# A recurrent layer on one core: key matrices before the small scales, an output projection in split fp16 products, and turns and updates moved or left out

## The reference

```
q, k, v = silu(conv4(xn @ Wq.T)), silu(conv4(xn @ Wk.T)), silu(conv4(xn @ Wv.T))   # 6 heads of 64
q, k = q / |q|, k / |k|                        # per head
beta = sigmoid(xn @ Wb.T);  g = -exp(A_log) * softplus(xn @ Wa.T + dt_bias)
per time step:  S = S * exp(g);  u = beta * (v - k S);  S = S + k^T u;  o = q S / 8
o = o * rsqrt(mean(o*o) + 1e-5) * o_norm_w * silu(xn @ Wg.T)
s = o @ Wo.T                                   # 384 -> 512, the output projection
f = relu(xn @ sign(up).T * up_scale) @ sign(down).T * down_scale * output_scale   # hidden 2048
x = x + s * silu(f)
```

## Time and profile before

| | us |
|---|---|
| median of 3 runs | 1397.91 (1397.85 to 1403.75) |
| the profiled execution's own time | 1397.27 |
| its span | 1395.2 |
| TensorE busy | 1330.5 (95%) |
| VectorE busy | 1065.5 (76%) |
| ScalarE busy | 734.8 (53%) |
| GpSimd busy | 524.1 (38%) |

### The profile page before, as it was taken

How to read it: one execution, slowest core, us unless ns; L and a number is a source line. 1 busy time by engine, 2 the same in 40 slices (tenths; PEclk the granted TensorE clock), 3 DMA queues, 4 the chain that set the end, 5 groups by cost and what they waited for, 6 DMA issues and landing times. The chain is left out here.

```text
span 1395.2 us, 24351 instructions
## 1 busy us (share of the span) xinstructions
PE 1330.5 (95%) x8972; PEld 652.9 (47%) x8972; DVE 1065.5 (76%) x1870; ACT 734.8 (53%) x1305; POOL 524.1 (38%) x434
## 2 busy tenths in 40 slices
PE   5888999999999999999999999999999999999998
PEld 2332333333333333333345548654585546755485
DVE  7889877787877887788857777597685886768855
ACT  5675666556655666566576423365134552354331
POOL 3599852112201321122215642176221753137331
PEclk9999999999999999999999999999999999999999
DMA  6420000000001000100460230102400013002211
GB/s 234 179 84 3 7 8 4 24 30 16 9 14 41 14 8 16 31 24 1 158 267 31 58 61 32 39 8 62 88 17 31 24 46 80 24 23 56 42 24 46
DMA packets 80469, 68.51 MB, mean 49 GB/s; under 512 B 46080, under 2 KB 67296, under 8 KB 77792
## 3 DMA queue, kind: packets, MB, share of 16 engines
q1 hardware_dynamic: 67936, 65.39, 15.2%
q10 hardware_dynamic: 12416, 1.57, 1.1%
HBM read 44.87 MB, written 17.87 MB: 45 GB/s over the span
## 5 line engine op out<-in xcount | busy, mean ns | idle before, releaser
L621 DVE TENSOR_REDUCE mS<-vpair 128x1 f16<-128x512 f32 x512 | 329.1, 686 | 112.8 <-PE vpair L1125 110.6
L936 ACT ACTIVATE probs<-bank 128x512 f16<-128x512 f32 x512 | 277.3, 595 | 163.4 <-PE bank L1132 163.1
L1179 PE MATMUL bank<-rows,both 128*128 128x512 f16 x1024 | 243.0, 380 | 0.4 <-DVE th L650 0.4
L436 POOL TENSOR_TENSOR h<-th,h 128x512 f16<-128x512 f32 x61 | 71.5, 1172 | 219.1 <-ACT h L907 219.1
L1179 PEld LDWEIGHTS bank<-rows,both 128*128 128x128 f16 x1024 | 91.3, 98 | 121.2 <-issue 15.5
L2156 PE MATMUL bank<-rows,both 128*128 128x512 f16 x512 | 117.2, 379 | 0.0
L1125 PE MATMUL vpair<-qk 32*128 32x512 f16 x512 | 99.9, 385 | 18.1 <-DVE mS L621 7.7
L2172 PE MATMUL bank<-both,hid 128*128 128x512 f16 x512 | 111.2, 379 | 0.0
L2140 PE MATMUL bank<-rows,both 128*128 128x512 f16 (+1 forms) x456 | 104.4, 379 | 0.9 <-PEq L160 0.9
L1132 PE MATMUL bank<-qv,qk 32*128 32x512 f16 x512 | 99.5, 385 | 0.0
L1193 PE MATMUL bank<-dn,h 128*128 128x512 f16 x256 | 98.0, 383 | 0.0
(11 more groups left out here) (334 smaller groups left out, 2671.9 us busy)
## 6 DMA issues: line engine op xcount, KB each, us to landing
h<-in_ug SPq DMA_DIRECT2D x8, 1024.0 KB, 5.3
lt_scratch<-big SPq DMA_DIRECT2D x16, 384.0 KB, 2.8
dn<-in_down SPq DMA_DIRECT2D x2, 2048.0 KB, 11.0
x_scratch<-th SPq DMA_DIRECT2D x16, 256.0 KB, 2.2
res<-x_scratch SPq DMA_DIRECT2D x16, 256.0 KB, 4.8
out_x<-res SPq DMA_DIRECT2D x16, 256.0 KB, 2.0
both<-in_w SPq DMA_DIRECT2D x2, 1548.0 KB, 10.4
t_scratch<-tok SPq DMA_DIRECT2D x16, 192.0 KB, 2.1
```

Source lines behind the costliest of these rows:

```text
L436: pool.tensor_tensor(h16(ft, 1), row32, h16(ft, 0), ALU.subtract).then_inc(S["row_lo"], 1)
L621: v.tensor_reduce(mS[:, u % 2, qt, 32 * j + DH:32 * j + DH + 1], SA[n % 2][:, :], AX.X, ALU.max).then_inc(S["max_done"], 1)
L936: a.activation(probs[:, n % (2 * G), :], SB[n % 2][:, :], ACT.Exp, scale=float(DH) ** -0.5).then_inc(S["p_ready"], 1)
L1179: mm = pe.matmul(GB[n % 2][:, :], w[:, kt, col:col + P], xnb(b, kt), start=r == 0, stop=r == 2 * KT - 1)
```

## The change

In the second layer:

1. `matrices("KK", 0)` runs on VectorE before the small scales instead of after them.
2. K and V of the first chunk are turned in step 0 after X5 instead of before Z. K of the last chunk is not turned or scaled, since
3. the state update after the last chunk (its decay, product and sum) is left out: nothing reads it.
4. The output projection: `wo1` is held as two fp16 halves of the scaled weights, and turned y as two fp16 halves, each projection is 9 fp16 products (high by high, high by low, low by high) instead of 3 fp32 ones. The high half of y is evicted by ScalarE, the low half by VectorE (`low_y`), so y's bank moves from ScalarE's rotation to VectorE's. A power-of-two scale for the weights is found in batch 0 on VectorE (`output_maxima`, `output_scales`, `output_low`), one TensorE product and two ScalarE operations. The weights' load is put into space of the hidden tile, and waits until the first layer's last rows are stored.

Two semaphores of the first layer are merged into others.

```diff
@@ bank_order
-        v += [(b, "bat")] + [(b - 1, "wo", TT - 1)] * (b > 0) + [(b, "ss")]
-        a += [(b, "ba"), (b, "pre", 0)] + [(b - 1, "yT", TT - 1)] * (b > 0)
+        v += [(b, "bat")] + [(b - 1, "yT", TT - 1), (b - 1, "wo", TT - 1)] * (b > 0) + [(b, "ss")]
+        a += [(b, "ba"), (b, "pre", 0)]
...
+            v += (tt > 1) * [(b, "yT", tt - 2)]
             v += (tt > 2) * [(b, "wo", tt - 3)]
-            a += (tt > 1) * [(b, "yT", tt - 2)]
-            v += rec * [(b, "SU", tt - 1)]
+            v += (rec and inv) * [(b, "SU", tt - 1)]
@@ layer1, SyncE
-            sp.dma_start(wo1[:, :, :], d["wo1"]).then_inc(S["wo_in"], 16)
+            sp.wait_ge(W["x1_last"], 32)
+            sp.dma_start(wraw, d["wo1"]).then_inc(S["wo_in"], 16)
@@ VectorE
+                def output_maxima():
+                    v.wait_ge(S["wo_in"], 16)
+                    v.tensor_reduce(wmax[:, 0:1], wraw, AX.XY, ALU.max, apply_absolute_value=True).then_inc(S["wo_r"], 1)
+                    v.tensor_reduce(wmax[:, 2:3], onw, AX.X, ALU.max, apply_absolute_value=True).then_inc(S["wo_r"], 1)
+
+                def output_scales():
+                    v.wait_ge(S["yh_r"], 1)
+                    v.wait_ge(S["wo_r"], 2)
+                    v.tensor_scalar(wmax[:, 1:3], wmax[:, 1:3], 1e-30, None, ALU.max).then_inc(S["wo_r"], 1)
+                    v.wait_ge(S["wo_r"], 3)
+                    v.tensor_scalar(wpow.bitcast(I32), wmax[:, 1:3].bitcast(I32), 0x7F800000, None, ALU.bitwise_and).then_inc(S["wo_r"], 1)
+                    v.wait_ge(S["wo_r"], 4)
+                    v.reciprocal(winv, wpow).then_inc(S["wo_r"], 1)
+                    v.tensor_scalar(wo_un, wpow[:, 0:1], wpow[:, 1:2], 0.5 / WO_TOP / Y_TOP, ALU.mult, ALU.mult).then_inc(S["wo_r"], 1)
+                    v.wait_ge(S["wo_r"], 5)
+                    v.tensor_scalar(wo_sc, winv[:, 0:1], WO_TOP, None, ALU.mult).then_inc(S["wo_r"], 1)
+                    v.tensor_scalar(y_sc, winv[:, 1:2], Y_TOP, None, ALU.mult).then_inc(S["wo_r"], 1)
+
+                def output_low():
+                    v.wait_ge(S["yh_r"], 2)
+                    v.wait_ge(S["wo_r"], WO_STEPS - 1)
+                    v.scalar_tensor_tensor(wo1[:, 1], wraw, wo_sc, wo1[:, 0], ALU.mult, ALU.subtract).then_inc(S["wo_r"], 1)
+
+                def low_y(n, rt):
+                    k = VI[n, "yT", rt]
+                    v.wait_ge(S["yh_r"], 2 + n * TT + rt + 1)
+                    v.scalar_tensor_tensor(yT[:, 1, :, rt * P:(rt + 1) * P], vbank[k % 3][:, 0:KW].rearrange("p (m c) -> p m c", m=MT), y_sc,
+                                           yT[:, 0, :, rt * P:(rt + 1) * P], ALU.mult, ALU.subtract).then_inc(S["v_took"], 1)
...
                 v.scalar_tensor_tensor(az, z[:, :, LH:], -1.0, z[:, :, LH:], ALU.mult, ALU.min).then_inc(S["az_r"], 1)
                 if b:
+                    low_y(b - 1, TT - 1)
                     gated(b - 1, TT - 1)
+                else:
+                    output_maxima()
                 conv(1)
...
                 for m in range(3, 7):
                     conv(m)
                     silu(m - 1)
+                    if b == 0 and m == 4:
+                        output_scales()
+                    if b == 0 and m == 6:
+                        output_low()
                 conv(7)
...
+                matrices("KK", 0)
                 v.wait_ge(S["v_took"], VI[b, "ss"] + 1)
                 v.reciprocal(rsk, ssq[:, :, LH:]).then_inc(S["small_r"], 1)
...
-                matrices("KK", 0)
                 matrices("KQ", 0)
...
+                    if tt > 1:
+                        low_y(b, tt - 2)
                     if tt > 2:
                         gated(b, tt - 3)
@@ ScalarE
+                def high_y(n, rt):
+                    k = VI[n, "yT", rt]
+                    a.wait_ge(S["v_full"], k + 1)
+                    a.activation(yT[:, 0, :, rt * P:(rt + 1) * P], vbank[k % 3][:, 0:KW].rearrange("p (m c) -> p m c", m=MT), ACT.Copy,
+                                 scale=y_sc).then_inc(S["yh_r"], 1)
...
+                if b == 0:
+                    a.wait_ge(S["wo_r"], WO_STEPS - 1)
+                    a.activation(wo1[:, 0], wraw, ACT.Copy, scale=wo_sc).then_inc(S["yh_r"], 1)
                 tanh_conv(5)
@@ TensorE, project_out
                     for m in range(MT):
-                        mm = pe.matmul(vbank[k % 3][:, :], yT[:, m, tt * P:(tt + 1) * P], wo1[:, m, :], start=m == 0, stop=m == MT - 1)
+                        for i, j in ((0, 0), (0, 1), (1, 0)):
+                            mm = pe.matmul(vbank[k % 3][:, :], yT[:, i, m, tt * P:(tt + 1) * P], wo1[:, j, m, :],
+                                           start=m == 0 and i == j, stop=m == MT - 1 and i == 1)
@@ TensorE, steps
                     if inv:
                         product_X5()
+                    if tt == 0:
+                        turn_kv()
...
-                    if rec:
+                    if rec and inv:
                         bk = vfill("SU", rt)
...
+                    if 0 < tt < TT:
+                        turn_kv()
                     if inv:
-                        turn_kv()
                         bk = vfill("Z", tt)
```

More of the change, by code:

```diff
@@ L1288 @@
 XRAISE, WRAISE = 64.0, 128.0
+WO_TOP, Y_TOP = 2.0 ** 14, 2.0 ** -10
+WO_STEPS = 9
+WO_COL = 3 * TT * LH
 def bank_order():
@@ L1713, in gated @@
                     v.wait_ge(S["g2_r"], n * TT + tt + 1)
-                    v.scalar_tensor_tensor(gate2(tt), split(vbank[k % 3][:, :]), 0.5, gate2(tt), ALU.mult, ALU.mult).then_inc(S["v_took"], 1)
+                    v.scalar_tensor_tensor(gate2(tt), split(vbank[k % 3][:, :]), wo_un, gate2(tt), ALU.mult, ALU.mult).then_inc(S["v_took"], 1)
                 def residual(n, tt):
@@ L1748, in _, with matrices @@
                     silu(m - 1)
+                    if b == 0 and m == 4:
+                        output_scales()
+                    if b == 0 and m == 6:
+                        output_low()
                 conv(7)
+                def matrices(nm, tt):
+                    dst = (LT if nm == "KK" else BT)[tt]
+                    for hf in range(2):
+                        v.wait_ge(S["GTm_r"], (b * TT + tt) * 2 + hf + 1)
+                        v.tensor_tensor(dst[:, hf:LH:2, :], mats(take(nm, tt, hf)), GT[tt % 2][:, hf:LH:2, :],
+                                        ALU.mult).then_inc(S["v_took"], 1)
                 bk = take("ss")[:, 0:TT * 2 * LH].rearrange("p (t c) -> p t c", t=TT)
@@ L1763, in _ @@
                 v.tensor_scalar(sn5[:, :, :], sn, rowm[:, 0:1], None, ALU.mult).then_inc(S["snm_r"], 1)
-                def matrices(nm, tt):
-                    dst = (LT if nm == "KK" else BT)[tt]
-                    for hf in range(2):
-                        v.wait_ge(S["GTm_r"], (b * TT + tt) * 2 + hf + 1)
-                        v.tensor_tensor(dst[:, hf:LH:2, :], mats(take(nm, tt, hf)), GT[tt % 2][:, hf:LH:2, :],
-                                        ALU.mult).then_inc(S["v_took"], 1)
                 def invert_blocks():
@@ L1874, in _ @@
                     if rec:
[L1876 to L1878 removed]
+                        k = b * KV + 2 * rt
+                        if inv:
+                            v.wait_ge(S["kv_full"], k + 1)
+                            v.tensor_tensor(heads(Kt), heads(fbank[0][:, 0:KW]), hb(vec[:, rt, LH:2 * LH], HD), ALU.mult).then_inc(S["kv_took"], 1)
+                            k += 1
+                        v.wait_ge(S["kv_full"], k + 1)
                         v.tensor_tensor(heads(Rv), heads(fbank[1][:, 0:KW]), hb(rvs[:, rt, :], HD), ALU.mult).then_inc(S["kv_took"], 1)
@@ L1922, in _ @@
                     if rec:
-                        v.wait_ge(S["ssS_r"], w + 1)
-                        v.tensor_tensor(S_[:, nxt, :, :], take("SU", rt)[:, 0:MT * HD].rearrange("p (h c) -> p h c", h=MT), ssS[:, :, :],
-                                        ALU.add).then_inc(S["v_took"], 1)
+                        if inv:
+                            v.wait_ge(S["ssS_r"], b * (TT - 1) + rt + 1)
+                            v.tensor_tensor(S_[:, nxt, :, :], take("SU", rt)[:, 0:MT * HD].rearrange("p (h c) -> p h c", h=MT), ssS[:, :, :],
+                                            ALU.add).then_inc(S["v_took"], 1)
                         v.wait_ge(S["osq"], w + 1)
@@ L1935, in _ @@
                 residual(b, TT - 2)
+            low_y(B - 1, TT - 1)
             gated(B - 1, TT - 1)
@@ L2028, in _ @@
                 tanh_conv(2)
+                if b == 0:
+                    a.activation(wmax[:, 1:2], take("vec")[:, WO_COL:WO_COL + 1], ACT.Copy).then_inc(S["yh_r"], 1)
                 a.activation(vec[:, :, :].rearrange("p t (i h) -> p i t h", i=3),
@@ L2152, in up_tile @@
                     else:
-                        past(pe, "kv_took", 2 * b * TT)
+                        past(pe, "kv_took", b * KV)
                     for kt in range(KT):
@@ L2177, in turn_y @@
                 def turn_y(n, rt):
```

(15 more changed lines are left out.)

50 lines of the change are left out of this document (24 added, 26 removed).

## The result

The changed kernel takes 1391.58 us (median of 7 runs, 1390.54 to 1394.60); the kernel before took 1399.89 beside it (7 runs, 1397.85 to 1403.75). The ratio is 0.9933, 95% interval 0.9918 to 0.9948: 0.7% or 8.3 us faster. The forecast was 12.2 us and 1385.7, with a range up to 1389.5: the direction was right, the time lies above the range. Of the 5.9 us between forecast and result 2.0 are the base (1399.89 instead of 1397.91 for the kernel before) and 3.9 are gain that did not come.

A forecast was written before the change was run, and what follows sets the result against it. TensorE, busy 95% of the span, was taken as the bound. Terms -10.3 - 2.0 - 1.6 - 5.1 + 1.6 + 3.3 + 0.5 + 1.4 = -12.2 us gave 1385.7 us; range 1381 to 1389.5, own range 1383 to 1388.5.

The forecast's parts named there:

- First chunk turned in the first step: Chunk step 0: six transposes move from before Z into TensorE's idle 0.55 us before Y5; taken as 0 a batch.
- Next x: Batch boundary: the next batch's first product newly waits for ScalarE's last turned copy, about 0.15 us x 3, +0.5.
- Preparation in batch 0: New VectorE maxima, tiny scale operations and low half of the weights delay batch 0; +1.6 us taken.
- rival B: Batch 0 preparation at its upper bound, each tiny operation waiting on GpSimd: +2.9, 1388.6 us; chance 0.12.
- The projections: Output projections on TensorE: 2.58 us becomes 1.94, gain 0.64 each, 16 of them, 10.3 us.
- the boundary waits: Batch boundaries: projection newly waits 1.1 us for VectorE's low half of y, 3 times, +3.3 us.
- the key matrices in batches 1 to 3: First key matrices masked ahead of the small scales: TensorE's wait goes, 1.7 us a batch, 5.1 us.
- the tail: After the last chunk: end moves 2.04 us earlier, so 1.4 of the 3.45 us priced there is not had.
- Rival C: Key wait only moves, KQ 0's masks coming as late as the old ones: +5.1, 1390.8 us; chance 0.08.
- D: No new waits, only a shorter TensorE queue; boundary, x and tail terms (5.2) fall away, 1380.5 us; chance 0.10.
- E: Low halves queue behind VectorE's next-x work, so TensorE waits at every turn of y: above 1405 us; chance 0.03.
- Rival F: Chunk steps are a VectorE and ScalarE chain; the 8.7 us taken from TensorE only opens idle time: 1394.4; chance 0.05.

The follow-up runs named there:

- best: Changed kernel with boundary projection after pre_tile(2), first chunk's K and V turned before Z again, idle products in the tail's two gaps; 1383.39 us, ratio 0.9871.
- best_low_later: best with the low half of the weights made after the second key matrices' masks in batch 0 instead of before conv(7); 1383.97 us, ratio 0.9865.
- again: The changed kernel, unaltered, run once more for a second trace; 1392.28 us, ratio 0.9943 to the kernel before.
- warm_tail: Changed kernel with idle TensorE products, 12 ahead of the last turn of y and 4 ahead of the last projection; 1390.39 us, ratio 0.9922.
- later: Changed kernel with the boundary's projection after pre_tile(2) instead of pre_tile(1), its gated eviction after conv(1); 1391.13 us, ratio 0.9920.
- no_split: Changed kernel without the fp16 split: output projection stays fp32 with 3 products, no preparation or low half; 1392.97 us, ratio 0.9939.
- turn_back: Changed kernel with the first chunk's K and V turned before Z again, as in the kernel before; 1388.11 us, ratio 0.9912.
- kk_only: Kernel before with only the first key matrices' masks moved ahead of the small scale operations on VectorE; 1392.64 us, ratio 0.9940.

## Why the prediction was too low

Forecast and measured change of each stage of layer 2 (forecast: the terms on record put where they fall; measured: the table):

```
                              forecast  measured
conv stretch, batch 0           +1.6     +0.55
chunk steps, batches 0 to 2     -8.0     -6.9
conv stretches, batches 1 to 3  -3.7     -3.6
last steps and tail             -2.05    +1.8
sum (of unrounded terms)       -12.2     -8.2
```

**The clock was the step that failed.** The prediction put it so: "the clock is already at its upper level (2.4 GHz), so nothing is to be had or lost there short of a fall that the slices before never show". The slices did not show it because one is 35 us wide; windows of 5 us show 0.69 at 780 to 785 us in the kernel before:

```profile
780.00:785.00 5.00, 5.00 (x23) 0.69 0.26 72
```

After the change two more falls stand in the last stage: 1.6 us in the steps and 1.9 in the last projection, 3.5 of the 3.8 us that this stage missed. Without them it would be 64.1, where 63.8 was forecast; in best and best_low_later it is 63.8 and 63.9. What the runs say of the cause: in the tail the last projection ran wholly or in most part at the lower clock (3.60 to 4.00 us of fp16, 4.51 of fp32) in 8 of 9 profiled executions in which its gaps stood open, in none of the 4 with idle products. In the first chunk step a fall came in 4 of 5 executions with the open gap of 0.86 us before Z (after, again, warm_tail, later; not in no_split), and in none of the 8 in which it was filled or was 0.55 us before Y5. In batch 0 it came in 6 of the 8 executions with the gap of 0.89 us before the squares (not in turn_back and later), behind the 1.75 us of the kernel before, and in none of the 4 with neither gap. Each of the four with a fall in the steps had it in one batch of four, though the gap is in every batch: an open gap goes with the fall, and something else decides whether it counts. What that is stays open. That idle time is the cause is shown in the tail, where idle products in the gaps were the only edit; in the steps it rests on fewer cases.

The Trainium skill's page TensorE: Matmul & The Clock Gate (Why this matters for your kernels) advises against long idle gaps of TensorE in mid-kernel because the clock goes down. These traces agree in direction but not in size: the gap that the page still allows is longer than any here (0.86 to 2.83 us), and the clock fell behind them all the same, so the measurement decides.

**First chunk turned in the first step: a term of 0, with bounds of -0.1 to +0.2.** It measured +0.2 a batch. The prediction weighed the six transposes against Z's wait for corner 6; but at 0.80 us they are longer than the idle 0.55 they were put into, so Y5 starts later, and behind it ScalarE's four copies set Z, in the kernel before too: there corner 6 was done at 1169.39 and the last copy, which the prediction did not look at, at 1169.56. The kernel before, then the changed one, whose Z starts at 1165.39:

```profile
1169.24 0.32 ACT L2100 ACTIVATE big<-bank 32x192 f32<-32x192 f32 x1
```
```profile
1164.97 0.32 ACT L2158 ACTIVATE big<-bank 32x192 f32<-32x192 f32 x1
```

The larger harm, the fall, came with the gap that this opened. (The prediction also called the wait for the masks the only one that comes back every batch; the wait of 0.55 for corner 5, four times, and short ones of up to 0.2 before S, twelve times, did too.)

**Next x.** Forecast 0.15 us, measured 0.39, three times (+0.7): the right wait, the size off.

**Preparation in batch 0.** Forecast +1.6 against the kernel before, measured +0.55. But the reference for the stage is not 106.12: with the masks ahead and no preparation it is 102.68. So the preparation costs 4.0 us gross, where my terms gave 3.3 (the 1.6 and the 1.7 of the key wait). Of the 4.0, 0.5 are the clock: in turn_back and later, without a fall, the stage is 3.5 above 102.68. So the size of the term was nearly right, and the net came out low because the kernel before had lost 1.6 us to a fall of its own there. The low half's place alone is 2.2 of the 3.5. I had costed it at VectorE's own pace and asked what VectorE was late for, which gave the masks; about half of the delay ran through GpSimd's squares instead. The sign named for it, a wait at the masks of more than 1.7 us in batch 0, did not show: it was 0.89 at the squares and 1.06 at the masks, the latter hidden in the changed kernel's own trace. The rule of GPSIMD Engine Reference in the Trainium skill, which the prediction set beside the terms, did bear on it: the low half reads two operands from SBUF, it took 2.71 us where 1.85 was possible, and GpSimd's squares 2.55 instead of 1.48. Its upper bound for the stage (+4.5, rival B) was far from reached.

**As forecast.** The projections (0.64 each), the boundary waits (1.08 against 1.1), the key matrices in batches 1 to 3 (1.65 alone against 1.7), the last update and K (neither stands in the last step's timeline any more), and the tail but for its clock. Rival C (the key wait only moves) fell with kk_only, D and E with the waits at L1743. Rival F is refuted where it was placed: the steps did get 2.3 us shorter a batch, of the 2.66 that the terms give.

**Of the whole change**, the masks of the key matrices are the bulk: 6.8 us of layer 2 in kk_only (5.0 in batches 1 to 3, 3.4 in batch 0, less 1.6 for the fall in the tail), against 8.2 for everything. The fp16 split, with 10.3 us the largest term, netted 3.1 alone and nothing on top of the others as built; with the boundary and the first step mended it brings 3.9, and with the low half moved 6.6 (653.0 against 646.4).

## What to carry to other kernels

Price a shortened instruction group together with the operations that feed it: here 9 fp16 products instead of 3 of fp32 saved 10.3 us over 16 projections and their preparation, low halves and waits took most of it back, until two of these were moved to a place where nobody waits.

Look at the granted clock in windows as short as the groups you price, before and after. An idle gap costs its own length and may cost more than that again in the products behind it (1.6 us behind 0.86); where it can't be closed, idle products that no one reads can fill it: here at a price of 0.1 us or less. A fall can also hide a wait, as in batch 0: before a wait is called gone, look whether the products ahead of it ran at full clock.

When two versions differ by less than the parts they share vary, compare stages of the traces and not spans: here a shared layer moved by 6 us while stages repeated to 0.05.

## What the runs showed of the hardware

TensorE's clock fell to the lower level behind gaps as short as 0.86 us (before Z) and 0.89 us (before the squares in batch 0), with small products behind them, and not every time: in 4 of 5 executions, in one batch of four, and in 6 of 8. The same gap sequence of 1.93 and 0.67 us in the tail left the clock alone in one execution (last projection 2.81 us) and halved it in another (4.51 us).

A VectorE operation over 128x1536 with both operands in SBUF took 2.71 us in one place and 1.85 in another, beside GpSimd in both, and GpSimd's products over 128x512 begun beside it took 2.55 and 2.68 us instead of 1.48 and of 1.2 to 1.6.

The first layer's end varied by 6.4 us over 13 profiled executions, and runs of one kernel by 8.4 us, the longer ones at the lower granted clock (0.990 against 0.997 over the run). In the stretch from 100 to 140 us the granted clock was 0.96 in the kernel before and 0.91 in the changed one and in best_low_later, in a stretch that the edits leave alone. Its cause wasn't looked for.
